# Throwaway TensorE products ahead of and between the first row turns of a mixture-of-experts stage

## The reference, cut to what matters

```python
probs = jax.nn.softmax(xf @ router_w.T, axis=-1)
topw, topi = jax.lax.top_k(probs, K)
...
keep = rank < capacity                       # the 560 heaviest of each expert
disp = jnp.zeros((E, capacity + 1, D), x.dtype).at[se, pos].set(xf[st])
...
g = jnp.einsum('ecd,edf->ecf', disp, wg)
u = jnp.einsum('ecd,edf->ecf', disp, wu)
eo = jnp.einsum('ecf,efd->ecd', jax.nn.silu(g) * u, wd)
out = jnp.zeros_like(xf).at[st].add(contrib)
```

## Time and profile before

| | |
|---|---|
| median of 3 runs | 3893.83 us (3892.44 to 3898.69) |
| the profiled execution | 3894.06 us, span 3892.3 us |
| mean granted TensorE clock | 0.977 |
| TensorE busy | 3675.3 us, 94% of the span |
| expert 0 starts | 2600.08 us |
| last product ends, near | 3872 us |

### The profile page before, as it was taken

The page is one execution under the profiler, slowest core; times in us unless marked ns, Lnnn a source line. Parts: engine busy times, 40 slices in busy tenths (PEclk is TensorE's granted clock), DMA queues, the critical chain, the costliest instruction groups (busy, mean ns, idle before and its releaser), DMA issues. The chain is left out here.

```text
span 3892.3 us, 84830 instructions
## 1 busy us (share of the span) xinstructions
PE 3675.3 (94%) x28086; PEld 3163.1 (81%) x28086; DVE 2410.9 (62%) x5661; ACT 1735.7 (45%) x4281; POOL 1264.2 (32%) x1192
## 2 busy tenths in 40 slices
PE   7999999999979999999999999749999999999998
PEld 6888888888778878877788878539899899899987
DVE  6888888888746676766667766465433434434343
ACT  4555545454445555555555555313333333333332
POOL 1333333333335555555555555410101101011010
PEclk9999999999989999999999999869999999999999
DMA  4222222222333343433433343222424324244232
GB/s 123 58 54 61 57 58 57 59 63 56 98 104 96 103 110 103 113 103 98 107 100 103 104 109 83 66 59 86 117 81 116 109 84 117 86 112 112 81 102 63
DMA packets 315532, 347.65 MB, mean 89 GB/s; under 512 B 45248, under 2 KB 232104, under 8 KB 315397
## 3 DMA queue, kind: packets, MB, share of 16 engines
q1 hardware_dynamic: 305796, 318.24, 30.3%
q0 software_dynamic: 9600, 27.58, 2.4%
HBM read 181.62 MB, written 38.65 MB: 57 GB/s over the span
## 5 line engine op out<-in xcount | busy, mean ns | idle before, releaser
L1559 DVE TENSOR_REDUCE x_mx<-x_psS 112x1 f32<-112x752 f32 x512 | 479.5, 936 | 421.2 <-PE x_psS L1127 415.6
L2278 DVE TENSOR_TENSOR hid<-e_psU,act_g 128x280 f32<-128x280 f32 x256 | 115.2, 450 | 687.6 <-PE e_psU L34 657.6
L1390 ACT ACTIVATE x_pt<-x_psE 125x448 f32<-125x448 f32 x768 | 389.5, 542 | 271.4 <-PE x_psE L1139 265.2
L1023 POOL TENSOR_TENSOR part<-x_pt 125x448 f32<-125x448 f32 x256 | 293.1, 1145 | 623.3 <-ACT x_pt L1390 622.8
L1921 POOL DMA_INDIRECT out<-ex_y,sidx x40 | 39.0, 976 | 1051.9 <-DVE ex_y L2311 1043.3
L612 POOL TENSOR_TENSOR qks<-qks,cos 128x448 f32<-128x448 f32 x128 | 148.7, 1161 | 674.7 <-DMA qks<-qk 674.7
L1127 PE MATMUL x_psS<-k_st,q_st 97*112 97x376 f32 x1024 | 289.4, 364 | 39.7 <-DVE x_mx L1559 26.2
L2067 ACT ACTIVATE act_g<-e_psG 128x280 f32<-128x280 f32 x256 | 103.7, 405 | 475.4 <-PE e_psG L34 457.8
L32 PE MATMUL e_psG<-ex_hi,g_hi 128*128 128x280 f32 x1024 | 303.4, 296 | 5.6 <-ACT act_g L2067 3.1
L32 PE MATMUL pj<-xT_hi,win_hi 128*128 128x224 f32 x1024 | 302.7, 296 | 1.7 <-DVE xT_lo L652 1.5
L32 PE MATMUL e_psU<-ex_hi,u_hi 128*128 128x280 f32 x1024 | 297.9, 291 | 2.9 <-issue 2.9
(11 more groups left out here) (281 smaller groups left out, 10751.3 us busy)
## 6 DMA issues: line engine op xcount, KB each, us to landing
k_st<-kT SPq DMA_DIRECT2D x768, 93.8 KB, 2.1
raw_g<-in_L_ffn_wg SPq DMA_DIRECT2D x128, 256.0 KB
raw_u<-in_L_ffn_wu SPq DMA_DIRECT2D x128, 256.0 KB
raw_d<-in_L_ffn_wd SPq DMA_DIRECT2D x128, 256.0 KB
qks<-qk SPq DMA_DIRECT2D x512, 56.0 KB, 2.0
q_st<-qT SPq DMA_DIRECT2D x384, 56.0 KB, 2.0
ctxt<-in_ctx SPq DMA_DIRECT2D x16, 1125.0 KB
xt<-in_x SPq DMA_DIRECT2D x16, 448.0 KB, 3.7
```

The source lines that it names most:

```text
L1023: pool.tensor_tensor(part[:], pt[j][:, 0, :], pt[j][:, 1, :], ALU.add).then_inc(parted, 1)
L1390: act.activation(pt[j][:, i, :], psE[(j + i) % 2][0:KR, 0:2 * T], ACT.Exp, scale=XD ** -0.5).then_inc(exp_done, 1)
L1559: dve.tensor_reduce(mx[:, j, h:h + 1], psS[0:HT, :, 0:376], AX.XY, ALU.max).then_inc(s_taken, 1)
L2278: dve.tensor_tensor(h[i][:, halves[s]], psU[:, 0:CH], act_g[i][:, halves[s]], ALU.mult).then_inc(S["mul"], 1)
```

## The change

Before the first turn TensorE now waits until `g_hi[0]` is written and then issues ten products of `same` (128x128) with `g_hi[0]` (128x512) into `e_psU`; after each of the five turns it issues one more. Nothing reads their result, and the first real product into `e_psU` starts a new sum.

```diff
+                def keep_awake(n):
+
+                    for _ in range(n):
+                        pe.matmul(psU[:], same[:], g_hi[0][:], start=True, stop=True)
+
                 def turn_first():
+                    pe.wait_ge(S["gu_hi"], 1)
+                    keep_awake(10)
                     for t in range(SLOT_TILES):
                         pe.wait_ge(first_rows[t], 16)
                         if t >= 2:
                             pe.wait_ge(S["x_lo"], t - 1)
                         for k in range(KD):
                             m = pe.transpose(psx[t % 2][:, k * HT:(k + 1) * HT], xg[:, t, k * P:(k + 1) * P], ident[0:HT, 0:HT])
                         m.then_inc(S["x_up"], 1)
+                        keep_awake(1)
```

## The result

| | median of 20 runs each | lowest to highest |
|---|---|---|
| before | 3895.36 us | 3890.28 to 3900.72 |
| after | 3890.78 us | 3885.88 to 3894.35 |

The ratio is 0.9985 with a 95% interval of 0.9979 to 0.9992: 0.15% faster, some 5.8 us (3.1 to 8.2) by the ratio and 4.6 by the medians. The forecast was 3891.9, 2.1 us of gain. The measured time lies in the range that was given, but the gain is more than twice the forecast one, and hardly any of it comes from where the forecast put it.

A forecast was written before the change was run, and what follows sets the result against it. TensorE, busy nearly all the time after 2600 us, was taken to pass any gain at its start to the end: 1.66 us at expert 0's first products plus 0.47 at the fifth turn, 2.1 off 3894.06, gives 3891.9 us, range 3889.8 to 3898.7.

The forecast's parts named there:

- the 2.1 us: Start of expert 0: total gain forecast from a full clock, 1.66 us at its first products plus 0.47 at the fifth turn.
- The costs of the products: Ahead of and between the turns: the added products cost nothing, the ten 4.2 us at low clock under 5.23 of cover.
- The fifth turn: Last row tile's transposes before expert 0: 0.55 us in place of 1.02 at full clock, 0.47 saved, all on the path.
- The first products: Start of expert 0: the first 15 products take 2.00 us in place of 3.66 at full clock, saving 1.66 us.
- The 55% for a full clock at 2600.08: Start of expert 0: chance given that TensorE's clock is at 2.4 GHz when the first gate product starts.
- Transposes and the clock: Turns ahead of expert 0: transposes help raise the clock, by a measured fall from 421 to 273 ns, against the skill page.
- Rival 2: Expert loops: added code moves later instructions, and the inner loop's 21 jumps back stall, losing 27 to 34 us; 3%.
- rival 3: Whole kernel: more than 0.2% faster, which would need stalls that go away; the three largest waits total 7.6 us; 3%.
- TensorE's waits after 2600 should be those of before: Expert stage: sign expected in the profile after; new issue waits in the loops would instead mean added code stalls jumps back.

The follow-up runs named there:

- 0 (again): The kernel before, unchanged, run again beside the first three variants for a second profile: 3901.64 us, ratio 1.0002.
- 0 (third): The kernel before, unchanged, a third time, on a third chip: 3896.76 us against 3896.66, ratio 1.0000.
- 5, between: The change without the ten products ahead of the first turn; the five behind the turns stay: 3906.16 us, ratio 1.0013 to the kernel before.
- 10, burst: The change without the products behind the turns; the ten ahead of the first turn stay: 3908.67 us, ratio 1.0018 to the kernel before.
- 10, early: The kernel before with ten 4-column products far ahead, in TensorE's wait for the routing's sorted weights: 3906.97 us, ratio 1.0015.
- 15, again: The changed kernel, unaltered, a second time on another chip: 3899.13 us against 3901.30 for the kernel before, ratio 0.9993.
- 15, third: The changed kernel, unaltered, a third time, on a third chip: 3889.60 us against 3896.66 for the kernel before, ratio 0.9984.
- 15, 4 columns: The change with its fifteen products 4 columns wide in place of 512: 3898.28 us against 3901.37 for the kernel before, ratio 0.9993.
- 15, early: The kernel before with fifteen 4-column products far ahead, in TensorE's wait for the routing's sorted weights: 3898.94 us, ratio 0.9993.
- 15, filled: The change with its fifteen products reordered: six ahead of the first turn, then 3, 1, 1, 1, 3 behind the turns: 3897.68 us, ratio 0.9988.
- 15, filled again: The reordered fifteen products (6, then 3, 1, 1, 1, 3) a second time, on a third chip: 3889.56 us, ratio 0.9980 to the kernel before.
- 128, early: The kernel before with 128 4-column products far ahead, in TensorE's wait for the routing's sorted weights: 3921.6 us in its one run.

## Why the prediction went as it did

In short: the 2.1 us were to come from the clock, and the change's first profile shows 0.2 us of them. The term that was put at nothing, the place of the outer loop, brought 2.9 us. That the time fell inside the range was luck.

All profiles beside each other. The gaps are from the start of the last product ahead of each to the start of the next; "E0" is from the first gate product to the first `ex_y` of expert 0:

| products added ahead of the loop | products from gap 1 to gap 2 | gaps at jump 1, us | gaps at jump 2, us | E0, us |
|---|---|---|---|---|
| 0 (before) | 12 | 0.67 + 1.89 | 1.25 + 1.62 | 168.36 |
| 0 (again) | 12 | 0.90 + 2.14 | 1.00 + 2.12 | 169.09 |
| 0 (third) | 12 | 0.82 + 1.51 | 0.64 + 1.57 | 168.41 |
| 5, between | 7 | 0.62 + 2.35 | 1.03 + 2.61 | 166.69 |
| 10, burst | 3 | 0.95 + 2.99 | 1.03 + 2.99 | 168.52 |
| 10, early | 3 | 1.00 + 2.45 | 1.18 + 3.27 | 168.58 |
| 15, the change | none | 1.35 | 1.10 | 168.22 |
| 15, again | none | 0.62 | 1.49 | 168.25 |
| 15, third | none | 0.63 | 1.33 | 168.27 |
| 15, 4 columns | none | 1.26 | 0.70 | 168.47 |
| 15, early | none | 1.04 | 0.98 | 169.18 |
| 15, filled | none | 0.78 | 1.72 | 166.74 |
| 15, filled again | none | 1.07 | 0.63 | 166.72 |
| 128, early | 12 | 0.87 + 1.84 | 0.58 + 1.84 | 168.90 |

**The costs of the products: right.** The burst took 4.51 us, ended ahead of the first tile, and in the first profile the turns started at the landings of their tiles or within 0.1 us. Nothing was lost by it.

**The fifth turn: the step failed.** "All on the path" was wrong. The transposes ran at the full clock in all three profiles of the change (0.60 or 0.61 us), and from the start of the fifth turn to the first gate product it was 2.34, 2.40 and 2.53 us, against 2.38 before: nothing arrived. I had followed the chain that ended last, in which DVE follows ACT, and had not asked what DVE does just ahead of it: a value table (L2242, L2234 in the kernel before) that now ends 0.45 us after ACT. The step needed DVE's rows between the turns.

**The first products: right in size, wrong in whether it happens.** The full clock at the start of expert 0 is worth 1.5 to 1.9 us (E0 of 166.7 against 168.2 to 168.6), where the forecast had 1.66. But in all three profiles of the change the clock was up when expert 0 started and fell 0.4 to 0.7 us into it, so E0 gained 0.1 to 0.2 us against two profiles of before and 0.8 to 0.9 against the third, in which the rise came later. The 55% for a full clock at 2600.08 asked the wrong question. What counts is whether it is held. The long burst goes with its loss: the variants without one (between, filled) hold the clock in all three profiles, the four profiles with the burst of ten at full width never do. The clean comparison, in which only the burst is taken out, rests on one profile; the filled order also adds two products ahead of expert 0.

**Transposes and the clock: the row was the right guide.** With one product between the turns the clock came up during the turns of the change at 2596.7, with transposes for more than half of the work, and the turns themselves shortened from 1.01 to 0.60 us. In the burst-alone variant, whose turns stood alone, it did not come back before 2605.6. The runs thus don't tell what transposes alone do; the opening of the kernel stays the row for that.

**Rival 2: its mechanism was true, with the other sign and at the other loop.** The prediction said "Nothing in the profile says that the place of the loop matters". Something did: two waits of `e_psU` on issue of 1.3 and 1.6 us, one behind each jump of the outer loop, 12 products into an expert. The code does wait for two semaphores there, but the profile finds neither late; and with 5 or 10 products added the gap stands between two products of one `unit`, where the code waits for nothing. The prediction had set these two waits beside the two jumps, and rival 3 had said that a larger gain needs stalls that go away, but neither asked what the added instructions do to them. In the change both are gone. Summed over both jumps, the gaps are 5.43, 6.16 and 4.54 us in the three profiles of before and 2.45, 2.11 and 1.96 in those of the change; with 0.13 of normal distance taken off each second gap, that is 2.9 us less on average. The same is in the variant with 4-column products and in the early one as well, and both measured 0.9993, some 2.7 us. This is the term that the sum lacked: "TensorE's waits after 2600 should be those of before" was the step that failed. The inner loop's 21 jumps, which the rival feared for, put no wait on issue into any profile's list of larger waits.

The traces show what the gaps wait for. They hold the transfers of instructions, 16384 bytes each, on a queue of their own; whose instructions they are the profile does not say. At every one of the 28 jumps in the table such a transfer lands 1.6 to 2.0 us before the first gap ends; at all 14 jumps with a second gap the next transfer lands 1.2 to 1.7 us before that gap ends (at the first jump of the first profile of before it runs from 3086.82 to 3088.00, and the gap ends at 3089.64). Where the second gap is missing, two transfers fewer are made in the whole program. The pages of before and of the change:

```profile
q8 instruction: 89, 1.46, 0.2%
q8 instruction: 87, 1.43, 0.2%
```

All three profiles of before and all with 5 or 10 products have 89, all seven with 15 products 87. So the transfers, whose landings go with TensorE's gaps, are TensorE's by all that the traces show.

The Trainium skill has the mechanism: "Runtime: NRT & Kernel Launch", Instruction fetch mechanics, says that instructions come in 16 KiB blocks of 256 and that a taken branch whose target is not in the window forces a fetch of its block before execution goes on. The first gap of every profile agrees, 0.6 to 1.7 us, and so do the size of the transfers and the return of the pattern with 128 products, 256 instructions; by itself that return would also fit blocks of a half or a quarter of the size. The page gives no price for the block behind the target's, which is the second gap, 1.5 to 3.3 us.

**The sum, by what was measured:** jumps 2.9, expert 0 with its start 0.1 to 0.9, together 3.0 to 3.8 us. The three measurements of the change are 0.9985, 0.9993 and 0.9984, which is 5.8, 2.7 and 6.2 us with intervals of 2 to 4 us to either side. The sum reaches into all three intervals, in the first and the third at their low end; where the other 2 to 3 us of those two come from stays open. Part of the scatter is known: the 2.9 us count the gaps alone. On the chip of the second measurement, 1.4 to 1.7 us returned as the wait on `hid` behind the first jump in all three profiles with 15 products. In the first profile of before, the late counts stood at the starts of experts 1, 2, 4, 6 and 7 and not at 3 and 5, which follow the jumps; a stall may hide such a wait, and its removal may bring it out. No profile of before from that chip is there to show it. The 8.0 us between the two first spans are no measure of the change: 4.7 us of them lie neither in the gaps (2.7) nor up to the end of expert 0 (0.6), but nearly all at the starts of the five experts whose waits on `act_g` the change's execution did not have. That execution was the second fastest of its 20. What makes those waits come and go was not tried.

## What to carry to other kernels

- A change that adds or takes away a few instructions ahead of a loop can move the loop in the blocks in which its instructions are fetched. Here that was worth from 3 us less to 7 us more, more than the work of the change itself. A control with the same number of instructions and no work, and one with the same number elsewhere, tells it apart. An issue wait a few products behind a jump back is the sign in the profile, and so is the count of instruction transfers, 89 against 87 here.
- Throwaway work that is to hold the clock belongs directly ahead of the dense work, in the gaps that it closes. A burst at the start of a thin stretch brings the clock up too early; here it was lost again twice, the second time 0.4 to 0.7 us into the real work.
- When a step on the critical chain is shortened, look at what the engines behind it do in that time. DVE had 0.12 us of slack between its filler and the `ex_lo` of the chain.

## What had not been expected of the hardware

- The second gap is a function of place, and it returns: it stands 12, 7 and 3 products behind the jump with 0, 5 and 10 products added, is missing with 15, and stands at 12 again with 128. Each product brings a weight load, so 5 products are 10 instructions, and the distance shrinks by 4 to 5 products for each 5 added. The nearer the second gap stands to the jump, the longer it is: 1.5 to 2.1 us at 12 products, 2.4 to 2.6 at 7, 2.5 to 3.3 at 3. That fits a transfer that is asked for at about the same time after the jump (0.2 to 1.2 us after the first gap's end) wherever its block begins.
- A stall of this kind can cost the clock as well. With 10 products added, in both variants and at both jumps, a first gap of about 1 us and a second of 2.5 to 3.3 us came with a stretch of 6.8 us at 1.2 GHz, which began in the second gap. Over 120 products behind each jump that is 2.5 us on top of the gaps (7.6 us more than before over both jumps, 2.5 of them in the gaps). With no product added the gaps never did this in three profiles; with 5 it happened at the second jump alone, behind gaps of 1.03 and 2.61 us.
- The products behind the turns kept the clock for expert 0 where the burst of ten ahead of them was missing, or cut to six with two more products behind the first and the fifth turn, and did not where it was there (0.4 to 0.7 us of full clock, then 3.4 us at half).
